# Causal attention stage: PSUM banks divided four and two instead of three and three

## What is computed

```
x = x + causal_attention(layernorm(x))
x = x + two_local_layers(layernorm(x))

def causal_attention(x):
    q, k, v = project(x)                      # 4 x 16 heads x 1024 x 16
    scores = q @ k.T / 4                      # 1024 x 1024 for each head
    attn = softmax(scores + causal_mask)
    return (attn @ v) @ wo + bo
```

## Time and profile before

| what | value |
|---|---|
| runs | 2340.26, 2348.76, 2340.21 us; median 2340.26 |
| profiled execution: its own time | 2343.61 us |
| profiled execution: span, first to last instruction | 2341.9 us |
| granted TensorE clock over the span | 0.951 of full |
| PE busy | 2007.6 us (86%) |
| DVE busy | 1458.2 us (62%) |
| ACT busy | 1243.1 us (53%) |
| POOL busy | 798.4 us (34%) |
| L717, exponentials, x768 | 330.1 us busy; idle before them 170.1 us, 169.8 of it until a score is there |
| L610, pieces, x768 | 243.7 us busy |
| L625, shifted scores, x768 | 243.0 us busy |
| L639, values, x1536 | 166.5 us busy |
| L762, masked reductions, x512 | 233.8 us busy |
| L765, plain reductions, x256 | 176.0 us busy |

### The profile page before, as it was taken

The page is one execution under the profiler, slowest core; times in us unless marked ns, Lnnn a source line. Parts: engine busy times, 40 slices in busy tenths (PEclk is TensorE's granted clock), DMA queues, the critical chain, the costliest instruction groups (busy, mean ns, idle before and its releaser), DMA issues.

```text
span 2341.9 us, 36128 instructions
## 1 busy us (share of the span) xinstructions
PE 2007.6 (86%) x11968; PEld 1252.2 (53%) x11968; DVE 1458.2 (62%) x3942; ACT 1243.1 (53%) x2980; POOL 798.4 (34%) x663
## 2 busy tenths in 40 slices
PE   5566899999987727999989989989989989989988
PEld 3232233333332525666666666656667667657656
DVE  5467788888873435646646646755745745746744
ACT  1121666666666315735745754753754754754663
POOL 2233322111231336415405505515604613613620
PEclk9896899999999868999999999999999999999999
DMA  5646844555620631000000000012100000000000
GB/s 146 151 131 137 148 96 70 78 82 82 108 93 20 168 119 77 1 27 10 1 28 10 1 24 14 1 66 85 29 19 19 19 19 18 19 13 25 19 1 27
DMA packets 124455, 128.97 MB, mean 55 GB/s; under 512 B 50460, under 2 KB 101232, under 8 KB 123248
## 3 DMA queue, kind: packets, MB, share of 16 engines
q1 hardware_dynamic: 123696, 117.75, 21.7%
q0 software_dynamic: 576, 8.91, 1.0%
HBM read 75.51 MB, written 50.86 MB: 54 GB/s over the span
## 4 chain that ended last, share of the span: by engine, by line
PE 35%; DVE 12%; ACT 8%; issue 6%; POOL 2%; DMA 0%; DVEq 0%; SPq 0%; POOLq 0%; ACTq 0%
DVE rot_s L1885 5%; PE qkv_ps L1395 5%; PE s_ps L1435 4%; PE qkv_ps L1336 4%; PE s_ps L1382 3%; PE s_ps L1516 3%; PE pt_ps L1448 3%; PE o_ps L1473 3%; DVE p_sb L1894 3%; ACT p_sb L1628 3%; POOL inv_norm L1779 2%; PE pt_ps L1435 2%; PE o_ps L1435 2%; PE pt_ps L1516 2%; PE o_ps L1516 2%
## 5 line engine op out<-in xcount | busy, mean ns | idle before, releaser
L717 ACT ACTIVATE probs<-st_ps 128x512 f32<-128x512 f32 (+3 forms) x768 | 330.1, 494 | 170.1 <-PE st_ps L625 169.8
L1336 PE MATMUL qkv_ps<-w_qkv,x_parts 128*128 128x512 f32 x1152 | 307.2, 410 | 33.9 <-DVE x_parts L1859 24.6
L1628 ACT ACTIVATE p_sb<-p_sb,negmax 128x256 f32<-128x256 f32 (+1 forms) x512 | 249.5, 490 | 72.8 <-DVE negmax L1894 72.7
L610 PE MATMUL s_ps<-k_stack,q_stack 96*128 96x512 bf16 (+3 forms) x768 | 243.7, 349 | 40.9 <-DVE piece_negmax L762 25.4
L762 DVE CUSTOM_DVE_ANT_0 seen<-s_ps,causal 128x128 f32<-128x128 f32 (+3 forms) x512 | 233.8, 484 | 45.8 <-PE s_ps L610 45.5
L625 PE MATMUL st_ps<-q_stack,k_stack 98*128 98x512 bf16 (+3 forms) x768 | 243.0, 337 | 14.5 <-ACT probs L717 10.1
L1336 PEld LDWEIGHTS qkv_ps<-w_qkv,x_parts 128*128 128x128 f32 x1152 | 210.8, 193 | 80.9 <-issue 39.7
L1894 DVE CUSTOM_DVE_ANT_0 p_sb<-s_ps,band 128x256 f32<-128x256 f32 (+1 forms) x512 | 185.4, 401 | 88.2 <-PE s_ps L1382 84.5
L1644 ACT COPY p_t<-pt_ps 128x512 f32<-128x512 f32 (+1 forms) x256 | 143.5, 561 | 160.7 <-PE pt_ps L1448 159.4
L1787 POOL TENSOR_TENSOR rot_c<-qn,turn_by 128x512 f32<-128x512 f32 x128 | 178.5, 1414 | 137.5 <-PE turn_ps L1362 111.6
L844 POOL TENSOR_SCALAR_AFFINE_SELECT probs<-probs 128x512 f32<-128x512 f32 x128 | 81.6, 637 | 419.1 <-ACT probs L717 419.1
(11 more groups left out here) (146 smaller groups left out, 3512.0 us busy)
## 6 DMA issues: line engine op xcount, KB each, us to landing
qk_scratch<-parts SPq DMA_DIRECT2D x64, 192.0 KB, 2.8
q_stack<-qk_scratch SPq DMA_DIRECT2D x96, 128.0 KB, 6.8
k_stack<-qk_scratch SPq DMA_DIRECT2D x96, 128.0 KB, 7.1
w_ffn<-ffn_weights POOLq DMA_DIRECT2D x4, 2176.0 KB, 11.5
v_scratch<-v_out SPq DMA_DIRECT2D x32, 256.0 KB, 2.6
v_sb<-v_scratch SPq DMA_DIRECT2D x16, 512.0 KB, 10.3
x_in<-xt_scratch SPq DMA_DIRECT2D x16, 512.0 KB, 4.1
ffn_weights<-w_high SPq DMA_DIRECT2D x2, 2176.0 KB, 8.0
```

What stands on the lines that cost most here:

```text
L610: pe.matmul(s_ps[i % 3][:, 0:kw], q_stack[0:STK, slot, h, qt * P:(qt + 1) * P], k_stack[0:STK, slot, h, k0:k0 + kw], start=True, stop=True ...
L717: act.activation(probs[:, n % 3, h, q0:CH], st_ps[i % 3][:, q0:CH], ACT.Exp).then_inc(exp_done.sem, 1)
L1336: mm = pe.matmul(qkv_ps[:, part * CH:(part + 1) * CH], x_parts[:, w % XR, xp, k, :], w_qkv[:, wp, k, part * INNER:(part + 1) * INNER], sta ...
L1628: act.activation(p_sb[:, u % 4, h, k0:PW], p_sb[:, u % 4, h, k0:PW], ACT.Exp, scale=-1.0, bias=negmax[:, u % 4, h:h + 1], accum_out=total[ ...
```

## The change

One more bank for the pieces and one less for the shifted scores. The scratch output `seen` of the masked reduction gets a fourth slot. A piece now waits for the reduction four pieces earlier, a score for the exponential two scores earlier. The order of the instructions on every engine is the same as before, row by row, and so are their number and shapes; only the semaphore values they wait for and the banks they name differ.

```
-        seen = sb("seen", [P, 3, CH])
+        seen = sb("seen", [P, 4, CH])
...
-        st_ps = [ps(f"st_ps{i}") for i in range(3)]
-        s_ps = [ps(f"s_ps{i}") for i in range(3)]
+        st_ps = [ps(f"st_ps{i}") for i in range(2)]
+        s_ps = [ps(f"s_ps{i}") for i in range(4)]
...
-        piece_done = count("piece_done", NP * HG, 3)
+        piece_done = count("piece_done", NP * HG, 4)
...
             def score_piece(group, i):
-                pe.wait_ge(piece_done.sem, when(piece_done, group, NP * HG, i - 3))
-                pe.matmul(s_ps[i % 3][:, 0:kw], q_stack[0:STK, slot, h, qt * P:(qt + 1) * P],
+                pe.wait_ge(piece_done.sem, when(piece_done, group, NP * HG, i - 4))
+                pe.matmul(s_ps[i % 4][:, 0:kw], q_stack[0:STK, slot, h, qt * P:(qt + 1) * P],
...
             def shifted_score(group, i):
-                pe.wait_ge(exp_done.sem, when(exp_done, group, NS * HG, i - 3))
-                pe.matmul(st_ps[i % 3][:, q0:CH], k_stack[0:STK + SHIFT, slot, h, kt * P:(kt + 1) * P],
+                pe.wait_ge(exp_done.sem, when(exp_done, group, NS * HG, i - 2))
+                pe.matmul(st_ps[i % 2][:, q0:CH], k_stack[0:STK + SHIFT, slot, h, kt * P:(kt + 1) * P],
...
-                act.activation(probs[:, n % 3, h, q0:CH], st_ps[i % 3][:, q0:CH], ACT.Exp).then_inc(exp_done.sem, 1)
+                act.activation(probs[:, n % 3, h, q0:CH], st_ps[i % 2][:, q0:CH], ACT.Exp).then_inc(exp_done.sem, 1)
...
-                    dve.tensor_tensor_reduce(seen[:, i % 3, 0:kw], s_ps[i % 3][:, 0:kw], causal[:, CH - kw:CH], -1.0, BIG,
+                    dve.tensor_tensor_reduce(seen[:, i % 4, 0:kw], s_ps[i % 4][:, 0:kw], causal[:, CH - kw:CH], -1.0, BIG,
...
-                    dve.tensor_reduce(result, s_ps[i % 3][:, 0:kw], AX.X, ALU.max, negate=True).then_inc(piece_done.sem, 1)
+                    dve.tensor_reduce(result, s_ps[i % 4][:, 0:kw], AX.X, ALU.max, negate=True).then_inc(piece_done.sem, 1)
```

## The result

The changed kernel takes **2364.93 us** (median of 7, 2358.22 to 2369.93), the kernel before beside it 2344.14 us (median of 7, 2337.12 to 2348.76). The ratio is **1.0095**, 95% interval 1.0079 to 1.0110: slower by 0.95%, or some 22 us (the two medians are 20.8 us apart). Forecast were +0.8%, a median of 2359.3 us, and a range of 2346 to 2369. The profiled execution took 2358.62 us with a span of 2356.9 us, which is at the fast end of the changed kernel's own spread and only 15.0 us over the span before.

The account below looks back on a forecast made before the run. No engine was taken as full; a ring of waits for banks bound the stage. Terms 8.8 + 0 + 1.7 + 2.5 + 1.2 + 4.8 = +19.0 us on the 2340.3 us median gave 2359.3 us, range 2346 to 2369.

Parts of the forecast that it names:

- The two-bank rule: With two score banks, a 512-wide set's third score goes at +1.15 us and its fourth at +1.64.
- The step from a set without pieces to the others: Score timing read in set 7 of the last group, applied to other sets: narrow fourth scores at +1.37, +1.15, +0.83.
- the new wait cannot be hidden: Claim that the lost score bank's wait stays exposed, since DVE and ACT are both fed from behind it.
- The walk: Set-by-set count of waits on TensorE's queue in an ordinary group (2 to 12): +0.80 us each, 8.8 in all.
- 0.24 given back in set 10, where PE waits for DVE's join anyway: Part of the +0.31 us for sets 9 to 11: +0.38 in set 9, -0.24 in set 10, +0.17 in set 11.
- Group 0: First group: costs nothing, since the next group's first score stands 2.24 us for a DMA.
- Group 13: Group with weight rounding: +2.5 us, of it +0.80 as an ordinary group and +1.7 for the late join.
- Group 14: Group without pieces in sets 10 and 11, hence 0.4 us less relief: +1.2 us.
- Group 15: Last group, without pieces or relief: every set's fourth score later, +4.8 us.
- Group 1: Group starting at half clock, with weight rounding: 0.4 + 1.25 + 0.06 = +1.7 us.
- The clock rival: TensorE's clock falls to half in one stretch of each of 15 groups: +61 us, 2420 us; chance 0.04.
- The rival with the larger gain: Fourth piece bank frees all 5.9 us a group of pieces' waits, held pieces of sets 5 to 8: 2305 us; chance 0.05.

Follow-up runs that it names:

- the moved pieces: Changed kernel with the pieces of sets 0, 1, 2, 4, 6 and 8 issued one score earlier; ratio 1.0038 to the kernel before.
- The later rounding: Changed kernel with ScalarE's weight rounding in groups 1 and 13 one exponential later; one execution of 2366.32 us.
- second profile: The changed kernel run again without any edit; 2365.05 us (median of 4), ratio 1.0098, profiled span 2368.1 us.
- filling: Changed kernel with three unread scores a set computed on TensorE in the last group; 2363.72 us (ratio 1.0107), again 2362.36 us (1.0097).

## Why the prediction was right, point by point

- **The two-bank rule.** Third score at the end of the first exponential plus 0.05 to 0.06 us, fourth at +1.64: measured +1.14 and +1.63 in set 7. The step from a set without pieces to the others held: the narrow sets 9, 2 and 3 have their fourth score at +1.36, +1.16 and +0.82 for +1.37, +1.15 and +0.83. That "the new wait cannot be hidden" was too strong: the moved pieces took 0.81 us a group off it.
- **The walk.** Every stretch came out within 0.04 us but one, sets 9 to 11. The step that failed is "0.24 given back in set 10, where PE waits for DVE's join anyway": set 10 gave back 0.07. The join's last step ends with GpSimd's triangle (L844), which starts after the fourth exponential of set 9, and that ends 0.15 us later in the set by the new wait. No run leaves the triangle out; that it holds the step is inferred from their ends, which lie within 0.03 us of each other before and after. Before, DVE's step of 0.49 us beside the triangle that started at 458.57:

```profile
458.57 0.64 POOL L844 TENSOR_SCALAR_AFFINE_SELECT probs<-probs 128x512 f32<-128x512 f32 x1 [1.93 <-ACT probs L717]
458.75 0.49 DVE L781 TENSOR_TENSOR negmax_parts<-negmax,negmax_parts 128x16 bf16<-128x16 f32 x1
```

after:

```profile
463.11 0.64 POOL L844 TENSOR_SCALAR_AFFINE_SELECT probs<-probs 128x512 f32<-128x512 f32 x1 [2.04 <-ACT probs L717]
463.13 0.64 DVE L781 TENSOR_TENSOR negmax_parts<-negmax,negmax_parts 128x16 bf16<-128x16 f32 x1
...
463.92 0.22 PE L615 MATMUL ot_ps<-ident_b,negmax_parts 128*32 128x128 bf16 x1
```

  The shift rows go 3.19 us after set 9's start, 3.04 before the change. In eleven groups that is 1.4 us missing from the sum.
- **Group 0** cost nothing, as said. **Group 13** +2.4 in the first profile and +2.1 in the second for +2.5, but by two misses that cancel: sets 4 and 5 are at +1.79 for my +1.25, since the join does end one GpSimd step later, and set 6 is at -0.72 for +0.06, because less of the half clock behind the rounding falls into it. The later rounding gives 2.16 us back and puts the join back in its step, which shows the mechanism of the +1.79. **Group 14** +1.1 for +1.2. **Group 15** +4.7 for +4.8 at full clock.
- **Group 1** is a term I had wrong: +1.7 forecast, 0.0 in the first profile and +3.1 in the second. Sets 0 to 3 ran at half clock at their start before the change (13.0 us) and in the second profile (13.4), and at full clock in the first (10.2). TensorE had stood 2.24, 1.93 and 0.06 us for the DMA ahead of them. Where the start is alike, before against second profile, sets 0 to 3 cost +0.42 for my +0.4, sets 4 and 5 +1.79 for +1.25, and sets 6 to 11 +0.87 for +0.06. There the half clock behind the rounding lasts 13.7 us for 10.2; the forecast had no term for that.
- **The clock rival** had 0.04, and I argued against it with a last group that "idles PE most of all, at a mean clock of 0.97". That argument failed, and the row did not carry it: before the change the clock was 1.00 from 725.9 to 754.4 and fell only behind the last score (751.38), so the 0.97 says nothing of the waits between scores. In the last group the granted clock fell to half, the 1.2 GHz level, in six of seven profiles with two score banks and no filling (33.9 to 38.3 us). With three score banks it stayed at full in three of four profiles (25.5 us) and fell for 3.4 us in the fourth (26.7). It fell in none of the ordinary groups 2 to 12 in any of the fourteen profiles; there the pieces take up much of the waiting. So the rival was right in one group of sixteen, and not as a stretch in each: worth 7 us in the second profile, and a likely part of why the medians differ by more than the first profile's 17.9 us. The Trainium skill, "TensorE: Matmul & The Clock Gate", section "A second HAM failure mode: psum-queue depth-cycling", warns of a clock that falls by waits for banks; the last group agrees with it, by 36.99 us against 30.14 for the same instructions, and the ordinary groups do not.
- **The rival with the larger gain** is refuted: the loads of pieces wait 10.1 us in place of 64.4, so 5 of the 5.9 us a group went, yet sets 5 and 7 are shorter by 1.03 us in all, and the fourth piece bank by itself is worth 0.81. That much of the loads' wait holds nobody was the reason given, and it held.
- **The nearness of the sum** is partly luck. The forecast change of 19.0 us meets 20.8 between the medians, but the ordinary groups cost 1.4 us more than forecast, group 1 costs 0.0 or 3.1 for 1.7, and the last group's clock, worth 7 us where it fell, was not in the sum. What was right by its reasons is the walk, wait by wait, of the ordinary group and of the last group at full clock.

## What to carry to other kernels

Two producers that share eight banks should be counted by where the wait stands in the shared queue and what stands behind it: here the third score bank is worth 1.74 us a group, since its wait stands before the end of all twelve sets; a fourth piece bank frees two places (0.81, with two score banks), a third one many (3.37, with three). A set without company (the last group) shows the rule bare and is the row to read first; a walk of one period then gives the sum to 0.13 us in 32. Where a wait is new, look for work to put in front of it, and check that what feeds the next engine does not pause meanwhile: pieces for VectorE, and scores whose exponentials GpSimd and the values need.

## What the runs showed of the hardware

- The release of a PSUM bank costs 0.05 to 0.06 us from the recorded end of the reader to the start of the waiting matmul, for ScalarE (L625, group 15, set 7: 0.06) and VectorE (L610, groups 2 to 12: 0.06) alike. From a matmul's start to the exponential's there are 0.49 us for the first score and 0.42 for the third, 512 columns wide, of set 7 in group 6, both with ScalarE waiting.
- A VectorE step of 128x8 or 128x16 values took 0.16 to 0.17 us alone and 1.37 to 2.47 us beside GpSimd's subtraction of 2.45 us a step, ending with it; a copy of 0.17 us that started about 0.05 us before such a step ended (at 681.47, group 13 of the changed kernel) was not held for the next. Reductions that read PSUM were not held: in group 1 of the kernel before, one of 512 columns took its usual time in the middle of the first GpSimd step, which began at 274.82:

```profile
275.24 0.68 DVE L762 CUSTOM_DVE_ANT_0 seen<-s_ps,causal 128x512 f32<-128x512 f32 x1
...
275.96 1.38 DVE L773 COPY negmax<-piece_negmax 128x8 f32<-128x8 f32 x1
```

  The Trainium skill, "SBUF — State Buffer", section "SBUF: two separate sides", has this as an exclusive lock of a shared port pair for whole instructions; these rows agree.
- The same instructions in the last group lasted 30.14 us at a granted clock of 1.00 and 36.99 us with half clock for part of it. That is 6.9 of the 11.2 us of span between the two profiles of the changed kernel, and group 1 has 3.1 more; both are places where TensorE waits. It does not account for the whole spread of executions, which was as wide with the last group filled.
